# The fusion MLP's operand h on one core: built by tokens and transposed by DMA, with u no longer transposed on TensorE

## The reference

```python
x = x + out_proj(attn_over_heads(k_proj(x)))       # modulated linears: w * style * demod, one set of weights per batch
h = ln(x, pw_g[pathway], pw_b[pathway]); h = ln(h, cp_g[c], cp_b[c])
t = ln(x, tm_g[c], tm_b[c]);  s = ln(x, ms_g[m], ms_b[m])
m, n, r = x + vec_m[batch], x + vec_n[batch], x + vec_r[batch]
cat = concat([w0*h, w1*t, w2*m, w3*n, w4*r, w5*s])  # 3072 features
x = x + ln(silu(cat @ int_W1 + int_b1) @ int_W2 + int_b2) * int_g + int_be
```

## Time and profile before

| | us |
|---|---|
| median of 3 runs | 857.05 (854.53 to 857.91) |
| the profiled execution | 856.02 |
| its span | 854.2 |
| PE busy | 818.0 |
| VectorE (DVE) busy | 652.6 |
| GpSimd (POOL) busy | 588.1 |
| ScalarE (ACT) busy | 497.5 |

### The profile page before, as it was taken

How to read it: one execution, slowest core, us unless ns; L and a number is a source line. 1 busy time by engine, 2 the same in 40 slices (tenths; PEclk the granted TensorE clock), 3 DMA queues, 4 the chain that set the end, 5 groups by cost and what they waited for, 6 DMA issues and landing times.

```text
span 854.2 us, 19739 instructions
## 1 busy us (share of the span) xinstructions
PE 818.0 (96%) x7482; PEld 684.3 (80%) x7482; DVE 652.6 (76%) x1077; ACT 497.5 (58%) x853; POOL 588.1 (69%) x763
## 2 busy tenths in 40 slices
PE   5996888999999999999999999999999999999996
PEld 5853766888888888888888888888888888888885
DVE  3589797779887878779888778779887877778652
ACT  3595646465756647465756647565756647564531
POOL 2279659767777766777777766767777766756462
PEclk9899899999999999999999999999999999999998
DMA  8973243435544342435444342425444342333210
GB/s 279 418 259 85 63 93 75 118 66 151 107 135 113 87 106 64 118 66 152 106 138 111 87 107 62 119 67 151 108 117 104 87 110 60 106 69 82 50 51 26
DMA packets 104366, 95.56 MB, mean 112 GB/s; under 512 B 72880, under 2 KB 78160, under 8 KB 102608
## 3 DMA queue, kind: packets, MB, share of 16 engines
q1 hardware_dynamic: 95056, 69.26, 30.9%
q0 software_dynamic: 4608, 16.78, 7.2%
q10 hardware_dynamic: 4608, 8.25, 2.9%
HBM read 69.60 MB, written 8.40 MB: 91 GB/s over the span
## 4 chain that ended last, share of the span: by engine, by line
PE 84%; DVE 5%; POOL 3%; ACT 3%; DMA 2%; issue 2%; ACTq 1%; SPq 0%; DVEq 0%; POOLq 0%
PE acc L414 39%; PE tok L414 29%; PE att L414 8%; PE xp L567 6%; PE xp L414 3%; DMA kb<-in_kb 1%; POOL raw_t L1778 1%; DVE stg_e L1345 1%; POOL Wol L1701 1%; DMA BD<-q 0%; ACT junk L979 0%; ACT BD L956 0%; DVE W1sl L1336 0%; DVE W1hl L1336 0%; SPq L311 0%
## 5 line engine op out<-in xcount | busy, mean ns | idle before, releaser
L1772 POOL TENSOR_TENSOR op1l<-ytmp,op1h 128x512 f16<-128x512 f32 x64 | 81.1, 1266 | 29.0 <-ACT op1h L932 28.6
L1719 POOL TENSOR_TENSOR xlo<-xraw,xhi 128x512 fp32r<-128x512 f32 x31 | 40.7, 1313 | 56.2 <-ACT xhi L822 56.1
L414 PE MATMUL acc<-op0h,W1xh 128*128 128x256 f32 x256 | 76.1, 297 | 1.2 <-DVE op0l L1437 1.2
L414 PE MATMUL acc<-op0l,W1xh 128*128 128x256 f32 x256 | 72.4, 283 | 0.0
L414 PE MATMUL acc<-op0h,W1xl 128*128 128x256 f32 x256 | 72.3, 282 | 0.0
L414 PE MATMUL acc<-op1h,W1th 128*128 128x256 f16 x256 | 69.8, 273 | 0.0
L414 PE MATMUL acc<-op2h,W1sh 128*128 128x256 f16 x256 | 69.8, 273 | 0.0
L414 PE MATMUL acc<-op1l,W1th 128*128 128x256 f16 x256 | 69.8, 273 | 0.0
L414 PE MATMUL acc<-op1h,W1tl 128*128 128x256 f16 x256 | 69.8, 273 | 0.0
L414 PE MATMUL acc<-op2l,W1sh 128*128 128x256 f16 x256 | 69.8, 273 | 0.0
L414 PE MATMUL acc<-op2h,W1sl 128*128 128x256 f16 x256 | 69.8, 273 | 0.0
(11 more groups left out here) (287 smaller groups left out, 2815.3 us busy)
## 6 DMA issues: line engine op xcount, KB each, us to landing
xsq<-in_x SPq DMA_DIRECT2D x32, 256.0 KB, 3.1
xb<-in_x SPq DMA_DIRECT2D x32, 256.0 KB, 3.1
out<-xb SPq DMA_DIRECT2D x32, 256.0 KB, 2.3
BD<-q SPq DMA_DIRECT2D x124, 64.0 KB, 2.1
BD<-v SPq DMA_DIRECT2D x124, 64.0 KB, 3.5
xraw<-in_xT SPq DMA_DIRECT2D x30, 256.0 KB, 3.0
ring<-in_k_wT ACTq DMA_DIRECT2D x6, 256.0 KB, 3.5
dmb<-dm_rows SPq DMA_DIRECT2D x6, 256.0 KB, 4.0
```

The costliest lines, as they stand in the source:

```text
L414: return e.matmul(o, a, b, start=start, stop=True, skip_group_check=True)
L1719: e.tensor_tensor(xlo[:, :, :], (xraw1 if g == 1 else xraw)[:, :, :], xhi[:, :, :].bitcast(F32), ALU.subtract).then_inc(s["xlo"], 1)
L1772: e.tensor_tensor(op_of[n]["l"][:, :, half(g)], four(ytmp[YT[n, g][0]]), op_of[n]["h"][:, :, half(g)], ALU.subtract).then_inc(s[f"o{n}l"], 1)
```

## The change

- `u_T` and `u_copy` go, with their uses of the xp banks. `product(g, "h")` multiplies u by tokens in pgb with gains by tokens.
- `gains(g, "h")` is one matmul of 512 columns with the one-hot matrix as weights, so its result has tokens on partitions.
- `prod_hi` and `prod_lo` of h write a pair fp of 128x2x512 fp16 (high, low). A new helper `turn(g)` in SP's list issues one DMA with `transpose=True` from fp (128x1024) to opT (128 x 8 x 128). W1 reads opT and waits for both tiles' DMAs (semaphores hD0, hD1). h has its own tiles now, so t's waits for h's readers go.
- opT lies where raw_s was, fp and a second pgb where raw_t was, since these raw weights are dead after the start. `gather` waits for the product two tiles earlier instead of for u_T.
- In SP's list turn(pa) and turn(pb) stand after load_sq, ahead of blocks_v(b), and load_ids moves behind blocks_v(b).
- On ScalarE silu(k-1, 1) moves ahead of value_low(b), and in passes with a modulation step prod_hi(pa, "s") ahead of a_hi(a). On VectorE silu_lo(k-1, 1) moves ahead of a_sum(b), and in pass 15 x_one(a) behind product(pb, "h"). On GpSimd gather(a) moves behind prod_lo(pb, "h"), and in pass 15 root1(a) too.

```diff
@@ -49,14 +49,14 @@
     yield from [("sty", 0), ("dm", 0), ("mr", 0), ("sty", 1), ("dm", 1), ("mr", 1), ("dr", 0)]
-    yield from [("a", 0), ("nb", 0), ("vT", 0), ("z", 0), ("a", 1), ("t", 0), ("x", 0), ("u", 0)]
+    yield from [("a", 0), ("nb", 0), ("vT", 0), ("z", 0), ("a", 1), ("t", 0), ("x", 0)]
     for k in range(1, NT):
         yield from [("x", pb), ("z", pb), ("t", pb)]
-        yield from [("s", pa), ("a", a), ("s", pb), ("h", pa), ("u", pb), ("h", pb), ("z", a)]
-        yield from [("t", a), ("u", a), ("a", b), ("x", a)]
+        yield from [("s", pa), ("a", a), ("s", pb), ("h", pa), ("h", pb), ("z", a)]
+        yield from [("t", a), ("a", b), ("x", a)]
     pa, pb = NG - 2, NG - 1
-    yield from [("x", pb), ("z", pb), ("t", pb), ("s", pa), ("s", pb), ("h", pa), ("u", pb), ("h", pb)]
+    yield from [("x", pb), ("z", pb), ("t", pb), ("s", pa), ("s", pb), ("h", pa), ("h", pb)]
 
@@ -166,10 +166,12 @@
         op = [{p: at(f"op{i}{p}", [128, 4, 256], F16 if i else F32R) for p in "hl"} for i in range(3)]
-        op_of = {"x": op[0], "t": op[1], "s": op[2], "h": op[1]}
+        op_of = {"x": op[0], "t": op[1], "s": op[2]}
+        opT = at("opT", [128, 2, 8, 128], F16, offset=place["raw_s"])
+        fp = [at(f"fp{i}", [128, 2, 512], F16, offset=place["raw_t"] + 2048 * i) for i in range(2)]
         zT = at("zT", [128, 4, 256])
-        uT = at("uT", [128, 4, 128])
-        pgb = at("pgb", [128, 1024])
+        kb2 = at("p_kb2", [128, 512])
+        pgb = [at("pgb0", [128, 1024]), at("pgb1", [128, 1024], offset=place["raw_t"] + 4096)]
         z = at("z", [128, 512])
@@ -252,7 +253,7 @@
             return {"sty": (s["styl"], i + 1), "dm": (s["dme"], i + 1), "mr": (s["dmb"], i + 1), "dr": (s["dmb"], 3), "vT": (s["LB"], 6), "nb": (s["nst"], 2),
-                    "a": (s["alo"], i + 1), "x": (s["oxl"], i + 1), "z": (s["zT"], i + 1), "u": (s["uT"], i + 1),
+                    "a": (s["alo"], i + 1), "x": (s["oxl"], i + 1), "z": (s["zT"], i + 1),
                     "t": (s["pt"], i + 1), "s": (s["ps"], i + 1), "h": (s["ph"], i + 1)}[n]
@@ -315,6 +316,15 @@
                     e.dma_start(BD[quad(i), :, quad(i), :, :], v12[quad(i), :, :, :, :]).then_inc(s["bv"], 16)
+
+            def turn(g):
+
+                if g > 1:
+                    e.wait_ge(s["W1h"], 2 * (g // 2))
+                else:
+                    e.wait_ge(s["wlx"], 2)
+                e.wait_ge(s["ohl"], g + 1)
+                e.dma_start(opT[:, g % 2, :, :], fp[g % 2][:, :, :].rearrange("p a b -> p (a b)"), transpose=True).then_inc(s[f"hD{g % 2}"], 16)
 
@@ -391,9 +401,12 @@
                     load_sq(b + 2)
+                turn(pa)
+                turn(pb)
+                if front:
+                    blocks_v(b)
+                if more:
                     load_ids(k + 1)
-                if front:
-                    blocks_v(b)
                 if more:
@@ -579,10 +592,6 @@
 
-            def u_T(g):
-                e.wait_ge(s["u"], g + 1)
-                transposed(("u", g), pgb, s["uTr"])
-
             def out_proj(g):
@@ -608,8 +617,11 @@
                     e.wait_ge(s["G"], "tsh".index(n) + 1)
-                for c in range(4):
-                    i = mm(o[:, c * 128:c * 128 + 128], GT[n][:, c * 128:c * 128 + 128], OH[(g // 2) % 2][:, half(g)], start=(c == 0))
+                if n == "h":
+                    i = mm(o[:, :], OH[(g // 2) % 2][:, half(g)], GT[n][:, :], True)
+                else:
+                    for c in range(4):
+                        i = mm(o[:, c * 128:c * 128 + 128], GT[n][:, c * 128:c * 128 + 128], OH[(g // 2) % 2][:, half(g)], start=(c == 0))
                 i.then_inc(s["G" + n], 1)
@@ -622,7 +634,6 @@
                 acc = ps[f"acc{pair}"]
-                o = op_of[n]
                 if n == "x":
@@ -630,7 +641,11 @@
                     e.wait_ge(*{"x": (s["wlx"], 1), "t": (s["wlp"], 1), "s": (s["wlx"], 2), "h": (s["wlx"], 3)}[n])
-                e.wait_ge(s["oxl" if n == "x" else f"o{n}l"], 2 * k + 2)
+                if n == "h":
+                    e.wait_ge(s["hD0"], 16 * k + 16)
+                    e.wait_ge(s["hD1"], 16 * k + 16)
+                else:
+                    e.wait_ge(s[f"o{n}l"], 2 * k + 2)
                 for j in js:
@@ -638,7 +653,11 @@
                             e.wait_ge(s["wlx"], 4)
-                        i = three(dst, W1[n, "h"][:, kt, ms], W1[n, "l"][:, kt, ms], o["h"][:, kt, :], o["l"][:, kt, :], n == "x" and kt == 0 and j == 0 and k < NT - 1)
+                        if n == "h":
+                            oh, ol = opT[:, :, kt, :], opT[:, :, 4 + kt, :]
+                        else:
+                            oh, ol = op_of[n]["h"][:, kt, :], op_of[n]["l"][:, kt, :]
+                        i = three(dst, W1[n, "h"][:, kt, ms], W1[n, "l"][:, kt, ms], oh, ol, n == "x" and kt == 0 and j == 0 and k < NT - 1)
                     if j == 1:
@@ -726,7 +744,6 @@
                     out_proj(a)
-                u_T(pb)
                 gains(pb, "h")
@@ -749,7 +766,6 @@
                     gains(a, "t")
-                    u_T(a)
                 W2_part(pa, (0, 1))
@@ -897,7 +913,7 @@
             def u_make(g):
-                pg = pgb[:, 0:512]
+                pg = pgb[g % 2][:, 0:512]
                 e.wait_ge(s["r2"], 4 * g + 4)
@@ -910,25 +926,24 @@
 
-            def u_copy(g):
-                e.wait_ge(s["uTr"], g + 1)
-                if g:
-                    e.wait_ge(s["ph"], g)
-                e.copy(uT[:, :, :], four(xp[XP["u", g][0]])).then_inc(s["uT"], 1)
-
             def prod_hi(g, n):
                 if n == "t" and k:
-                    e.wait_ge(s["W1h"], 2 * k)
+                    e.wait_ge(s["W1t"], 2 * k)
                 elif n == "t" and g == 0:
                     e.wait_ge(s["dmW"], 16)
+                elif n == "h" and k:
+                    e.wait_ge(s[f"hD{g % 2}"], 16 * k)
                 elif n == "h":
-                    e.wait_ge(s["W1t"], 2 * k + 2)
+                    e.wait_ge(s["wlp"], 1)
                 e.wait_ge(s["p" + n], g + 1)
+                if n == "h":
+                    e.copy(fp[g % 2][:, 0, :], ytmp[YT[n, g][0]][:, :]).then_inc(s["ohh"], 1)
+                    return
                 e.copy(op_of[n]["h"][:, :, half(g)], four(ytmp[YT[n, g][0]])).then_inc(s[f"o{n}h"], 1)
@@ -1111,11 +1125,14 @@
                     split_hi(WL["2", "h"], raw["2"], s["wh"])
+                if mod:
+                    prod_hi(pa, "s")
                 if mod or k == 1:
                         mod_hi(*mod, (2, 3))
-                prod_hi(pa, "s")
+                if not mod:
+                    prod_hi(pa, "s")
                 u_make(pb)
@@ -1130,7 +1147,6 @@
                 prod_hi(pa, "h")
-                u_copy(pb)
                 prod_hi(pb, "h")
@@ -1156,8 +1172,9 @@
                     u_make(a)
+                silu(k - 1, 1)
+                if front:
                     value_low(b)
-                silu(k - 1, 1)
                 if k == 1:
@@ -1166,11 +1183,9 @@
                         prod_hi(a, "t")
-                        u_copy(a)
                         a_hi(b)
                         a_hi(b)
-                        u_copy(a)
                         prod_hi(a, "t")
@@ -1426,7 +1441,7 @@
                 e.wait_ge(s["v"], 2 * g + 2)
-                e.bn_stats(stB, pgb[:, 0:512]).then_inc(s["a2"], 1)
+                e.bn_stats(stB, pgb[g % 2][:, 0:512]).then_inc(s["a2"], 1)
                 e.wait_ge(s["a2"], 2 * g + 1)
@@ -1445,10 +1460,13 @@
                 y = take_y(e, (n, g))
-                src, ready = (uT[:, :, :], s["uT"]) if n == "h" else (zT[:, :, half(g)], s["zT"])
                 e.wait_ge(s["G" + n], g + 1)
-                e.wait_ge(ready, g + 1)
-                e.tensor_tensor(four(y), src, four(xp[XP[n, g][0]]), ALU.mult).then_inc(s["p" + n], 1)
+                if n == "h":
+                    e.wait_ge(s["u"], g + 1)
+                    e.tensor_tensor(y[:, :], pgb[g % 2][:, 0:512], xp[XP[n, g][0]][:, :], ALU.mult).then_inc(s["ph"], 1)
+                    return
+                e.wait_ge(s["zT"], g + 1)
+                e.tensor_tensor(four(y), zT[:, :, half(g)], four(xp[XP[n, g][0]]), ALU.mult).then_inc(s["p" + n], 1)
 
@@ -1604,8 +1622,11 @@
                     v_T(b)
+                    if more:
+                        x_one(a)
+                product(pb, "h")
+                if front and not more:
                     x_one(a)
-                product(pb, "h")
                 if k == 1:
@@ -1625,11 +1646,11 @@
                 silu_lo(k - 1, 0)
+                silu_lo(k - 1, 1)
                 if front:
                     product(a, "t")
-                silu_lo(k - 1, 1)
                 if more:
@@ -1744,15 +1765,17 @@
             def gather(g):
-                if g:
-                    e.wait_ge(s["uTr"], g)
+                if g > 1:
+                    e.wait_ge(s["ph"], g - 1)
```

(38 more changed lines are left out.)

## The result

| | before | after |
|---|---|---|
| median of 6 runs each, in turns | 855.43 us (853.50 to 857.91) | 864.86 us (863.49 to 870.31) |
| ratio to before, 95% interval | | 1.012 (1.009 to 1.016) |
| profiled execution, its span | 856.02, 854.2 | 864.49, 862.7 |

The account below looks back on a forecast made before the run. TensorE was taken as the bound, busy 818.0 of 854.2 us. From the profiled 856.02, less 11.6 for removed transposes, plus 4.7 of stall, came 849.1, stated as 849.0; 8-in-10 range 843.5 to 866.

Parts of the forecast that it names:

- Part 1: Transposes of u removed from TensorE: 0.44 and 0.36 us a group, 11.6 us saved in passes 2 to 16.
- Part 2: Gains of h by tokens: four matmuls of 128 columns become one of 512, 0.20 against 0.21 us, nothing either way.
- Part 3: Transposing DMAs of h added, W1h waits where they outlast the windows from prod_lo: 4.7 us of stall.
- L: Time from the start of a transposing DMA's issue to its landing, taken as 3.8 us.
- The formula: TensorE's stall at W1h: 3(L - 3.0) + 4(L - 3.45) + (L - 2.9) + 7(L - 5.2), only positive terms; 4.7 us.
- the windows: Time from prod_lo(pb, "h") ending to W1h's first matmul: 5.2, 3.0, 3.45 or 2.9 us by kind of pass.
- The rival that bears the forecast's opposite: Transposes outlast the windows at W1h: slower by over 0.5% from L = 5.2, 866 at L = 5.6; chance 0.27.
- something on top: Unsized addition to the load's 3.1 us, for small turned writes and the gather right behind on the same DMA engines.
- Its lower bound: Least landing time of the transposing DMA, that of an ordinary 256 KB load: 3.1 us.
- Part 5: Orders and buffers: gather and affine end long before their reader; silu(1) ahead of value_low(b) delays a_sum(b); nothing counted.
- Part 4: SP's queue: two more DMAs a pass; values(b) covered up to 2.8 us of queue time, scores 0.6 left, no stall.
- k = 1: First loop pass: TensorE's wait for the first product of h goes, VectorE's chain behind it stays; nothing counted.

Follow-up runs that it names:

- e5: Changed kernel with no turning DMA issued; W1's part for h reads a constant operand without waiting for turned h, so h is left out; 846.97 us.
- e4: Changed kernel with gather(a) moved behind true_scale(b) in GpSimd's order, 1 to 4 us later; 913.92 us.
- e2: Changed kernel with the same 256 KB DMA from fp to opT as a plain copy, so h enters W1 unturned; 854.07 us.
- e1: Changed kernel, but W1's part for h reads a constant operand and doesn't wait for the turning DMAs, which still run; 864.16 us.
- e10: e1 with v_stats(a) moved behind e_second(b) on VectorE and u_make(a) behind the silus on ScalarE; 850.25 us.
- e11: Changed kernel, whole, with v_stats(a) moved behind e_second(b) on VectorE and u_make(a) behind the silus on ScalarE; 863.80 us.
- e8: Changed kernel with product(pb, "h") ahead of x_one(a) on VectorE, root1(a) behind both low halves of h on GpSimd, gather ahead of them; 863.64 us.
- e9: e8 with score_low(b) ahead of z_make(a) on ScalarE in every pass; 852.79 us.
- e7: Changed kernel with product(pb, "h") ahead of x_one(a) on VectorE, root1(a) behind both low halves of h on GpSimd, gather behind them; 876.84 us.

## Why the prediction was wrong

- **Part 1, the removed transposes: right, a little low.** A plain pass that doesn't wait is 46.8 us and not 47.7 (e5), 0.9 where 0.80 was priced. **Part 2** is inside that.
- **Part 3, L: mis-sized, and this is one half of the failure.** Taken 3.8, measured 3.1 alone and 5.4 in the median of the second turns, for which W1h waits. The formula was sound: at 5.4 it gives 3 x 2.4 + 4 x 1.95 + 2.5 + 7 x 0.2 = 18.9 us, and 856.0 - 11.6 + 18.9 = 863.3 against the 864.5 of the profiled run. That agreement is partly luck: PE's wait was 14.4, not 18.9, and the rest came from the other chain. The formula charges passes 15 and 16 with 4.5 us at that L, but there the turn landed in 3.1 and 3.2 and PE waited 1.1; and in passes 7 and 8 the second turn was issued 0.6 and 0.4 us sooner than the windows had it (23.73 us into pass 7, reckoned 24.34). The rival that bears the forecast's opposite (break-even at L = 4.7) was therefore the right one in its place and near in its price, but not in its mechanism. The blocks do not cost 0.64 us each in a row; a 128 x 1024 turn takes 3.1 us, and the gather issued right behind it holds back its completion (3.2 us in the median of e4, where no gather is near). The prediction saw this neighbour, and let it weigh as "something on top". Its lower bound, the 3.1 us of a load, was met by chance: the plain copy between the same tiles lands in 2.4 (e2).
- **Part 3 also booked a gain without its price.** That prod_lo no longer stands behind the gather was counted as 1.1 us of window. The gather then starts 1.2 us later (21.8 us into a plain pass, before 20.6), which was costed at nothing.
- **Part 5, "both end long before their reader": the step that fails outright.** The affine's reader on DVE is v_stats, with e_second and so values(b) queued behind it. Before, POOL already waited 13.1 us for gathers and DVE 8.4 for the affine: there was no long slack. The affine begins 26.0 us into a plain pass before, 27.9 to 29.3 after; in e5 it begins at up to 27.6 with no wait of PE in those passes. e1 shows what this alone does: with the whole L stall gone, the kernel is still at 864.2. And with a DMA that lands in 2.4 us and never keeps W1h waiting, e2 is at 854.1, no faster than before: even a right L would not have made the forecast of a faster kernel come true.
- **Part 4 held in the main.** SP is held 1.28 us by each turn, 3.6 for both in pass 8 with the wait between; the trace has no wait of values(b) for BD. The scores waited for it, 1.1 us in all (0.8 in pass 5, a plain pass, where 0.6 us were reckoned left), before 0.5; e5, without turns, has 1.5, so this need not be the turns' doing. That issue takes more than twice a plain one (0.52) was not foreseen, and didn't matter.
- **k = 1.** The prediction counted nothing; pass 2 starts 2.05 us sooner (148.32, before 150.37), of which 1.85 were there when pass 1 began (92.25, before 94.10).
- **L by the pages.** The Trainium skill (Advanced Engine Details and Errata, X-Bar Transpose (TRN2)) has transposing DMAs as fast as ordinary ones. The runs don't agree: with the same tiles the plain copy lands in 2.4 us (e2), the turn in 3.1 alone, and only the turn is held back by the gather. The Trainium skill (VectorE: DVE Perf Modes, The three transpose paths) gives 1309 ns for one 128x128 block by DMA. Here eight blocks land in 3.1 us, 0.39 a block, so the prediction rightly did not multiply that figure by eight; no run turns a single block.

So two steps failed: L, 5.4 us and not 3.8, and the path gather, affine, v_stats, e_second, priced at nothing. The cause is settled by the square of e1, e10 and e11 for the two chains, and by e4 and e5 for what the two kinds of DMA do to each other. Left open is why the completion of a turn is late once its packets are through, and why it is not in pass 1; no run separates that.

## What to carry to other kernels

Two waits in one pass of a pipeline cover each other: the profile shows the first in full and only the remainder of the second, so removing the first alone may give nothing. Ask of each transfer that starts later who reads it, and what stands behind that reader in its engine's list; the price is paid there. When an order is changed for one engine, look at each in-order list that takes its result (here ACT's z ahead of the scores), since a wait there (3.4 us in the rows of e8) moves the softmax too.

## What the runs showed of the hardware

- A transposing DMA of 128 partitions x 2 KB: 1024 packets of 256 bytes, 1.4 us of packets, 3.1 us to landing, 1.28 us of SP. The plain copy: 2.4 us and 0.52 us.
- A gather of 512 KB issued 0.1 us behind it (144 packets in its queue) stretches the turn's landing to 5.4 us in the median, and the gather's own from 5.0 (e5) to 6.4 us; in pass 1 the turn's landing stayed at 3.1. With the gather 2.4 us ahead of the first turn (e8, e9), the turns land in 3.8 to 3.9 in the median. The plain copy is not held back, and the gather behind it lands in 5.5 (e2).
- A wait of PE can cost more than its length. Waits of 2.1 us in passes 3 and 7 of the changed kernel left the granted clock at 1.00. In pass 3 of e1, behind a wait of 4.75 us, the granted clock fell, and the windows read (us, then PE's busy time, the clock in the third column from the end):

```profile
222.00:232.60 10.60, 5.85 (x55) 5.08 (x54) 3.82 (x8) 4.14 (x6) 3.07 (x4) 0.94 0.77 110
232.60:240.00 7.40, 7.40 (x52) 6.32 (x53) 4.02 (x7) 4.25 (x9) 6.56 (x10) 0.62 0.24 38
```

A mean of 0.62 is mostly the lower of the two levels (1.2 of 2.4 GHz). That pass took 54.93 us, in e5 49.55, of which 3.1 are longer waits (5.05 against 1.95): some 2.3 us are the clock's. e7 shows it too: passes 5 and 9 have nearly the same waits (0.76 and 0.68 for the e split, 1.11 for silu) and take 51.0 and 49.0 us; only in pass 5 did the clock fall (0.75). The stretch around those waits in either:

```profile
331.70:337.00 5.30, 4.19 (x43) 3.47 (x44) 2.81 (x6) 5.15 (x11) 1.00 (x4) 0.75 0.33 52
```
```profile
532.50:538.00 5.50, 4.34 (x49) 3.71 (x50) 3.00 (x6) 5.24 (x11) 1.20 (x4) 1.00 0.32 51
```
